# Dense attention of a two-layer block: six matmuls of the identity with residual columns, ahead of the first transposed scores

## The chip, the cores and the metric

The kernel runs as one program on one core of a Trainium2 chip. The metric is the device time of one execution, in microseconds (us). Lower is better. The engines named below are PE (TensorE, the matrix multiplier; PEld is its weight load), DVE (VectorE), ACT (ScalarE), POOL (GpSimd) and SP (SyncE, which here only issues transfers).

## The reference

The program computes two pre-normalised layers on `x` of shape 4 x 1024 x 256: a windowed attention, a mixture of gated experts, a dense attention with a norm behind it, and a mixture with Sinkhorn gates. The change lies in the second attention, which is

```python
def _L1_attn_ref(x, wq, bq, wk, bk, wv, bv, wo, bo, gamma, beta):
    H, D = 16, 16
    Q, K, V = x @ wq + bq, x @ wk + bk, x @ wv + bv
    Q = Q.reshape(B * H, S, D)      # K and V likewise
    scores = jnp.einsum('bqd,bkd->bqk', Q, K) / jnp.sqrt(jnp.float32(D))
    attn = jax.nn.softmax(scores, axis=-1)
    ctx = jnp.einsum('bqk,bkd->bqd', attn, V).reshape(B, S, E)
    out = ctx @ wo + bo + x
    ...
```

The reshape cuts the 1024 x 256 matrix into 16 groups of 64 rows, so that each of the 64 groups (4 x 16) is an attention of 1024 positions with head size 16, without a mask.

## The kernel before, in words

Each part of the network is a phase: a set of programs, one for each engine, that meet only at semaphores. `group_attention` (line 1656) is the phase of the change. Queries and keys come from `project_groups` by way of device memory, as a rounded part and a rest, and stand in SBUF stacked on 48 rows (`ST`) for each of two halves of the 128 partitions (`HR`, 64).

The work is cut into 512 units (`UNITS`: 32 blocks of `UB` = 16). One unit is 128 queries of one group against its 1024 keys. It is handled twice:

- As **scores** (`scores`, line 1885): two matmuls of 48 rows, 128 columns of weights and 512 moving columns, one for each half of the keys. They fill one of two slots (`b_s`, 1024 columns of PSUM each). DVE takes the maximum over the 1024 columns (line 1811). `slot_of` (line 1871) makes PE wait until DVE has read the slot's previous use, two uses ago. After 16 units DVE transposes the block's maxima (line 1818), and SP and POOL copy them by small DMAs into one more row of the queries (lines 1758 and 1790).
- As **transposed scores** (`scores_T`, line 1893): the same products with the keys as weights and 49 rows, the extra row being the negated maxima. The result lies in one of three PSUM banks (`b_t`, `RING` = 3). ACT takes the exponential of it (line 1845), and `weigh` (line 1906) multiplies the values with it: four matmuls of 256 columns, each on 32 columns of the array.

PE's order is written out by the loop at line 1953. At step `s` it does the scores of unit `s`, and the transposed scores of unit `back = s - LAG` with `LAG` = 26. The weighing begins at `back` = 4:

```python
if s < UNITS:
    scores(s, 1).then_inc(use_done, 1)
if 0 <= back < UNITS:
    scores_T(back, 1)
if 4 <= back <= UNITS + 3:
    weigh(back // 2 - 2, back % 2)
```

So steps 0 to 25 hold scores alone, steps 26 to 29 hold scores and transposed scores, and from step 30 on there is the weighing too. At a few places of each pair of blocks (step 65 is the first) `context` and `project` add transposes and a projection, which use the slots as well. Two matmuls of different halves of the rows, a unit's scores and another's transposed scores, run at the same time when they stand next to one another in the order, which is why the order alternates them.

The operands of the added matmul exist already: `g.ident` is the 128 x 128 identity and `g.x` the residual, 32 tiles of 256 columns, both of type fp32. `b_t[s % RING]` is a bank that nothing has used yet at these steps.

Of the kernel before, what the change touches and what calls it, by code (L numbers as in the profile page):

```python
# [54 lines left out]
@contextmanager  # L55
def phase(nc):

    sems = []
    with ExitStack() as e:  # L64
        def semaphore(name):
            sem = e.enter_context(nc.semaphore(name))
            sems.append(sem)
            return sem

        def begin():  # L70
            def start(eng, share):
                for sem in share:
                    eng.sem_clear(sem)
                for sem in share:
                    eng.sem_inc(sem, ONE)

            with nc.Block() as block:  # L77
                @block.sync
                def _(sp):
                    start(sp, sems[0::4])  # L80

                @block.scalar
                def _(act):
                    start(act, sems[1::4])

                @block.vector
                def _(dve):
                    start(dve, sems[2::4])

                @block.gpsimd  # L90
                def _(pool):
                    start(pool, sems[3::4])
            return e.enter_context(nc.Block())

        yield e, semaphore, begin
# [526 lines left out]
def normalised_tiles(nc, g, gate, gate_b, logits, rows_out, xnT_out, shared):  # L622
# [3 lines left out]
    C, HALVES = 4, 2  # L626
    STEPS, TH = T // C, C // HALVES
    with phase(nc) as (e, semaphore, begin):
# [21 lines left out]
        def _(sp):  # L650
# [4 lines left out]
            shared.load_weights(sp, g.ins, 0, shared_in)  # L655
            for i in range(STEPS):
                sp.wait_ge(xn_ready, ONE + C * (i + 1))
# [5 lines left out]
                if i:  # L663
                    sp.wait_ge(lo_ready, ONE + HALVES * i)
                    sp.dma_start(xnT_out[i - 1], parts[:, :, :, C * P * (i - 1):C * P * i].bitcast(F32)).then_inc(parts_kept, 16)
            sp.wait_ge(lo_ready, ONE + HALVES * STEPS)
            sp.dma_start(xnT_out[STEPS - 1], parts[:, :, :, C * P * (STEPS - 1):].bitcast(F32)).then_inc(parts_kept, 16)
            sp.wait_ge(shared_in, ONE + 16 * shared.LOADS)
            sp.wait_ge(chunks_in, ONE + 16 * 2)
            sp.wait_ge(parts_kept, ONE + 16 * STEPS)  # L670
            for u in range(2):
                sp.wait_ge(rows_kept[u], ONE + 16 * (STEPS // 2))

# [982 lines left out]
def group_attention(nc, g, parts, values, qs, ks, v):  # L1656
# [9 lines left out]
    LAG = UB + 10  # L1666
    SETS = 3
    RING = 3
# [2 lines left out]
    RB = UB // 2  # L1671
    CONTEXT_AT, TURN_AT, PROJECT_AT = 7, 13, 18
    LATE = BLOCKS // 2 - 2
    STEPS = UNITS + LAG + UB + 20

    def block_of(b):
# [2 lines left out]
    def score_unit(s):  # L1679

        b, j = s // UB, s % UB
        c, gp, hf = block_of(b)
        return c, j % 2, 2 * gp + j // 2 // HQ, HQ * hf + j // 2 % HQ
# [6 lines left out]
    def step_uses(s):  # L1690

        uses = [("scores", s)] if s < UNITS else []
        pair, at = (s - LAG) // (2 * UB) - 1, (s - LAG) % (2 * UB)
        if 0 <= pair < BLOCKS // 2:
            uses += [("context", pair)] * (at == CONTEXT_AT) + [("project", pair)] * (at == PROJECT_AT)
        return uses

    def transposed_context(back):

        return back // (2 * UB) - 1 if back > UB and back % (2 * UB) == TURN_AT else None  # L1700
# [11 lines left out]
    with phase(nc) as (e, semaphore, begin):  # L1712
# [17 lines left out]
        b_s, b_t, b_o = g.bank2[0:2], g.bank[4:4 + RING], g.bank[7]  # L1730
# [62 lines left out]
        def _(dve):  # L1793
# [6 lines left out]
            def statistics(m):  # L1800
                for t in (first_tile(m), first_tile(m) + 2):
                    nc.vector.bn_stats(g.stats[:, t, :], g.x[:, t, :]).then_inc(stats_ready, 1)

            for s in range(STEPS):
                for kind, arg in step_uses(s):
# [19 lines left out]
                    elif kind == "project":  # L1825
                        t = first_tile(arg)
                        both = g.x[:, t:t + 3:2, :]
                        nc.vector.tensor_tensor(both, slot[:].rearrange("p (h n) -> p h n", h=2)[:, :, 0:D], both, ALU.add).then_inc(use_read, 1)
                        if arg >= LATE:
                            dve.wait_ge(use_read, ONE + use + 1)  # L1830
                            statistics(arg)
                if UNITS <= s < UNITS + LATE:
                    m = s - UNITS
# [36 lines left out]
        def _(pe):  # L1870
            def slot_of(use):
                if use >= 2:
                    pe.wait_ge(use_read, ONE + use - 1)
                return b_s[use % 2]
# [10 lines left out]
            def scores(s, kh):  # L1885

                c, h, n, q = score_unit(s)
                a, rows = c % SLOTS, slice(HR * h, HR * h + ST)
                slot = b_s[use_place["scores", s] % 2]
                return nc.tensor.matmul(slot[:, HALF * kh:HALF * (kh + 1)], qs[a][rows, n, P * q:P * (q + 1)],  # L1890
                                        ks[a][rows, n, HALF * kh:HALF * (kh + 1)], start=True, stop=True)

            def scores_T(back, n):

                w, b, j = 2 * back + n, back // UB, back % UB
                c, gp, hf = block_of(b)
                a, h, kt = c % SLOTS, 1 - j % 2, j // 2
                rows = slice(HR * h, HR * h + ST + 1)
                if j == 0 and n == 0:
                    pe.wait_ge(max_in[0][b % 2], ONE + MAX_IN * (b // 2 + 1))  # L1900
                    pe.wait_ge(max_in[1][b % 2], MAX_IN * (b // 2 + 1))
                bank = ring_bank(ring_place["weights", w])
                nc.tensor.matmul(bank[:], ks[a][rows, 2 * gp + n, P * kt:P * (kt + 1)],  # L1903
                                 qs[a][rows, 2 * gp + n, HALF * hf:HALF * (hf + 1)], start=True, stop=True).then_inc(sT_done, 1)

            def weigh(k, half):

                b, kt = k // RB, k % RB
                c, gp, hf = block_of(b)
                first = HALF // 2 * half  # L1910
                cols = slice(first, first + HALF // 2)
                if kt == 0 and half == 0:
                    pe.wait_ge(o_ready, ONE + b)
                    if b % 4 == 0:
                        pe.wait_ge(v_in[c % SLOTS], ONE + V_IN * (c // SLOTS + 1))
                pe.wait_ge(exp_ready, ONE + NG * (k + 1))
                for h in range(2):
                    for n in range(2):
                        at = BL * (2 * h + n)
                        last = nc.tensor.matmul(b_o[at:at + BL, cols], v[c % SLOTS][:, h, 2 * gp + n, kt, :],  # L1920
                                                probT[k % SETS][2 * h + n][:, cols], start=(kt == 0 and first == 0),
                                                stop=(kt == RB - 1 and first > 0), skip_group_check=True)
                last.then_inc(pv_done, 1)
# [10 lines left out]
            def context_T(m):  # L1934
                bank = ring_bank(ring_place["contextT", m])
                pe.wait_ge(use_read, ONE + use_place["context", m] + 1)
                for n in range(NG):
                    last = nc.tensor.transpose(bank[:, P * n:P * (n + 1)], ctxn[:, n].rearrange("p q d -> p (q d)"), g.ident[:])
                last.then_inc(cT_done, 1)
# [13 lines left out]
            for s in range(STEPS):  # L1953
                back = s - LAG
                if s < UNITS:
                    c = s // (4 * UB)
                    if s == 2 * UB:
                        pe.wait_ge(qk_in[0], ONE + FIRST_IN)
                    elif s % (4 * UB) == 0 and c > 0:
                        first = FIRST_IN if c % SLOTS == 0 else QK_IN  # L1960
                        pe.wait_ge(qk_in[c % SLOTS], ONE + first + QK_IN * (c // SLOTS))
                    slot_of(use_place["scores", s])
                    scores(s, 0)
                if 0 <= back < UNITS:
                    scores_T(back, 0)
                if s < UNITS:
                    scores(s, 1).then_inc(use_done, 1)
                if 0 <= back < UNITS:
                    scores_T(back, 1)
                if 4 <= back <= UNITS + 3:  # L1970
                    weigh(back // 2 - 2, back % 2)
                for kind, arg in step_uses(s):
                    if kind != "scores":
                        other[kind](arg)
                if transposed_context(back) is not None:
                    context_T(transposed_context(back))
# [484 lines left out]
```

## Time and profile before

| what | value |
|---|---|
| median of 3 runs | 2432.5 us |
| the runs | 2428.86, 2432.5 and 2436.8 us |
| profiled execution, its own time | 2439.18 us |
| its span, first to last instruction | 2437.2 us |
| mean granted clock of PE | 0.908 |
| PE busy | 2024.1 us, 83% of the span |
| DVE busy | 1630.2 us, 67% |
| ACT busy | 1116.2 us, 46% |
| the phase of the change | 1375.7 to 2124 us |

A granted clock of 1.00 stands for 2.4 GHz and 0.50 for 1.2 GHz. The busy time of PE counts each matmul with its latency, and overlapping matmuls once. So a PE shown as busy for the whole of a stretch can still have gaps in which no column goes through the array. An fp32 matmul shows up as two MATMUL records.

### The profile page before, as it was taken

How to read it: one execution, taken by the hardware profiler on the slowest of the kernel's cores; microseconds unless marked ns; L12 is line 12 of the kernel's file. 1: busy time of each engine (PE TensorE's matmuls, PEld its weight loads, DVE VectorE, ACT ScalarE, POOL GpSimd, SP SyncE). 2: the span in 40 equal slices, each digit the busy share in tenths (PEclk: the TensorE clock that was granted, in tenths of full speed). 3: DMA queues.
4: the chain of work that ended last, by engine and by line, in shares of the span. 5: the costliest groups of instructions: out<-in, count | busy, mean ns of one | idle time of the engine just before them, and what ended most of it. 6: DMA issues, size and time to landing. Idle time of an engine off the chain costs nothing. (4 is left out here: it accounts for less than half of the span.)

```text
span 2437.2 us, 51300 instructions
## 1 busy us (share of the span) xinstructions
PE 2024.1 (83%) x18407; PEld 1393.6 (57%) x18408; DVE 1630.2 (67%) x2834; ACT 1116.2 (46%) x2169; POOL 452.3 (19%) x608
## 2 busy tenths in 40 slices
PE   2888888669979999989968899999999999835052
PEld 2766766448879999988857533434334343324042
DVE  3666666556735555546644579999999999386953
ACT  1555545333223333332223158888888888611010
POOL 2101001010011111114434112112221122030036
PEclk9999999889989999999989769999999999955566
DMA  2000000192151111113339777745755900031036
GB/s 87 2 0 0 0 0 0 60 336 80 35 182 47 47 47 47 47 43 106 109 114 271 201 51 72 67 46 52 49 47 47 71 2 2 5 104 35 0 112 200
DMA packets 207045, 172.15 MB, mean 71 GB/s; under 512 B 121740, under 2 KB 184808, under 8 KB 204744
## 3 DMA queue, kind: packets, MB, share of 16 engines
q1 hardware_dynamic: 187448, 131.64, 27.8%
q0 software_dynamic: 17744, 26.26, 4.0%
q10 hardware_dynamic: 1728, 12.58, 1.4%
q8 instruction: 79, 1.29, 0.3%
q14 instruction: 46, 0.38, 0.1%
HBM read 106.30 MB, written 63.84 MB: 70 GB/s over the span
## 5 line engine op out<-in xcount | busy, mean ns | idle before, releaser
L1811 DVE TENSOR_REDUCE ga_nmax<-banks 128x1 fp32r<-128x1024 f32 x512 | 615.5, 1219 | 39.8 <-PE banks L1890 38.4
L1845 ACT ACTIVATE ga_probT<-banks 128x512 f32<-128x512 f32 x1024 | 556.7, 597 | 157.6 <-PE banks L1903 105.9
L1890 PE MATMUL banks<-a_ks,a_qs 48*128 48x512 f32 x1024 | 392.3, 466 | 9.3 <-PEq L77 5.3
L1903 PE MATMUL banks<-a_qs,a_ks 49*128 49x512 f32 x1024 | 381.8, 453 | 0.0
L1920 PE MATMUL banks<-ga_probT,a_v 128*32 128x256 f32 x4096 | 332.9, 398 | 6.4 <-ACT ga_o L1851 6.4
L1890 PEld LDWEIGHTS banks<-a_ks,a_qs 48*128 48x128 f32 x1024 | 159.4, 195 | 225.2 <-DVE ga_nmax L1811 158.3
L1321 PEld LDWEIGHTS banks<-rb_xT,rb_own_w 128*128 128x128 f32 x2272 | 267.1, 193 | 8.3 <-issue 3.7
L1321 PE MATMUL banks<-rb_xT,rb_own_w 128*128 128x128 f32 x2272 | 267.9, 276 | 4.1 <-DMA rb_w<-in_L_ffn_rw_dram 3.5
L1790 POOL DMA_DIRECT2D a_qs<-ga_max_rows x256 | 130.8, 519 | 580.6 <-DVE ga_max_rows L1818 539.4
L1296 ACT ACTIVATE rb_silu<-banks,rb_own_b 128x128 f32<-128x128 f32 x284 | 80.9, 367 | 254.9 <-PE banks L1321 254.9
L1920 PEld LDWEIGHTS banks<-ga_probT,a_v 128*32 128x32 f32 x4096 | 81.6, 108 | 198.3 <-ACT ga_probT L1845 151.2
L1101 PE MATMUL banks<-m_xnT,sh_w 128*128 128x512 f32 x768 | 185.0, 400 | 6.4 <-DVE sh_w L896 5.3
L1101 PEld LDWEIGHTS banks<-m_xnT,sh_w 128*128 128x128 f32 x768 | 146.3, 193 | 39.7 <-issue 9.3
L1903 PEld LDWEIGHTS banks<-a_qs,a_ks 49*128 49x128 f32 x1024 | 154.8, 189 | 10.1 <-ACT ga_probT L1845 8.8
L1213 POOL DMA_INDIRECT rb_xb<-normalised_rows,m_source x71 | 67.3, 948 | 467.5 <-PE banks L1315 319.3
L346 DVE TENSOR_REDUCE wa_nmax<-banks 128x4 f32<-128x512 f32 x128 | 86.9, 679 | 97.3 <-PE banks L543 97.3
L1246 DVE SCALAR_TENSOR_TENSOR rb_gluT<-banks,rb_own_b,rb_silu 128x128 f32<-128x128 f32 x284 | 79.9, 344 | 91.8 <-PE banks L1321 91.8
L1343 PE MATMUL banks<-rb_w,rb_gluT 128*128 x568 | 135.6, 382 | 1.4 <-DVE rb_gluT L1246 1.4
L414 ACT ACTIVATE wa_probT<-banks 128x512 f32<-128x512 f32 x128 | 76.4, 597 | 130.6 <-PE banks L555 130.6
L1343 PEld LDWEIGHTS banks<-rb_w,rb_gluT 128*128 128x128 f32 x568 | 103.3, 192 | 12.9 <-issue 1.6
L555 PE MATMUL banks<-ident,wa_prob 128*128 128x128 f32 x512 | 85.8, 291 | 25.1 <-ACT wa_prob L407 25.1
L407 ACT ACTIVATE wa_prob<-wa_ex 128x512 f32<-128x512 f32 x128 | 80.5, 629 | 51.1 <-DVE wa_ex L348 50.1
(288 smaller groups left out, 3031.7 us busy)
## 6 DMA issues: line engine op xcount, KB each, us to landing
m_xnT<-xnT_parts ACTq DMA_DIRECT2D x12, 1024.0 KB, 4.8
sorted_out<-rb_yb SPq DMA_DIRECT2D x71, 128.0 KB, 1.7
xnT_parts<-np_parts SPq DMA_DIRECT2D x8, 1024.0 KB, 9.2
m_w<-in_L_ffn_rw_dram SPq DMA_DIRECT2D x2, 4096.0 KB, 21.6
values<-pg_v SPq DMA_DIRECT2D x16, 512.0 KB, 3.1
a_v<-values SPq DMA_DIRECT2D x16, 512.0 KB, 9.1
a_qs<-queries_rounded SPq DMA_DIRECT2D x28, 256.0 KB, 8.5
a_ks<-keys_rounded SPq DMA_DIRECT2D x28, 256.0 KB, 9.6
```

The lines of the kernel that those rows point to most:

```text
L346: nc.vector.tensor_reduce(nmax[k][:], sc, axis=AX.X, op=ALU.max, negate=True).then_inc(max_ready, 1)
L555: last = nc.tensor.transpose(b_pt[k][:, P * j:P * (j + 1)], prob[k][:, j, :], g.ident[:])
L1101: last = nc.tensor.matmul(bank[m % 2][:], w[a][:, k, P * m:P * (m + 1)], xnT[s][:, b, k, :], start=(k == 0 and a + b == 0), stop=(k == KD ...
L1296: last = nc.scalar.activation(silu[:, m, :], b_p1[:, P * m:P * (m + 1)], ACT.Silu, bias=own_b[s][:, 0, m:m + 1])
L1321: last = nc.tensor.matmul(bank[:, P * m:P * (m + 1)], w[:, k, P * m:P * (m + 1)], xT[s][:, k, :], start=(k == 0), stop=(k == KD - 1))
L1343: last = nc.tensor.matmul(b_y[:, 0:D], gluT[:, m, :], flat[:, bass.ds(n * KH + m, 1), :].rearrange("p o d -> p (o d)"), start=(m == 0), st ...
L1790: nc.gpsimd.dma_start(dst, src).then_inc(max_in[1][b % 2], 16)
L1811: nc.vector.tensor_reduce(nmax[b % 2][:, at:at + 1], slot[:], axis=AX.X, op=ALU.max, negate=True).then_inc(use_read, 1)
L1845: nc.scalar.activation(probT[k % SETS][2 * h + n][:], b_t[ring_place["weights", w] % RING][:], ACT.Exp, scale=SCALE).then_inc(exp_ready, 1)
L1890: return nc.tensor.matmul(slot[:, HALF * kh:HALF * (kh + 1)], qs[a][rows, n, P * q:P * (q + 1)], ks[a][rows, n, HALF * kh:HALF * (kh + 1)] ...
L1903: nc.tensor.matmul(bank[:], ks[a][rows, 2 * gp + n, P * kt:P * (kt + 1)], qs[a][rows, 2 * gp + n, HALF * hf:HALF * (hf + 1)], start=True, ...
L1920: last = nc.tensor.matmul(b_o[at:at + BL, cols], v[c % SLOTS][:, h, 2 * gp + n, kt, :], probT[k % SETS][2 * h + n][:, cols], start=(kt == ...
```

## The change

At each of the steps 20 to 25 (`LAG - BUSY <= s < LAG`), behind the second half of the scores, PE multiplies the identity by 512 columns of the residual, in fp32, into the bank `b_t[s % 3]`. No semaphore is attached. The bank is overwritten later by transposed scores, and nothing reads what the matmul wrote. The results are the same.

```diff
@@ -1671,6 +1671,7 @@
     RB = UB // 2
     CONTEXT_AT, TURN_AT, PROJECT_AT = 7, 13, 18
     LATE = BLOCKS // 2 - 2
+    BUSY = 6
     STEPS = UNITS + LAG + UB + 20
@@ -1965,6 +1966,8 @@
                     scores_T(back, 0)
                 if s < UNITS:
                     scores(s, 1).then_inc(use_done, 1)
+                if LAG - BUSY <= s < LAG:
+                    nc.tensor.matmul(b_t[s % RING], g.ident[:], g.x[:, 0:2, :].rearrange("p t d -> p (t d)"), start=True, stop=True)
                 if 0 <= back < UNITS:
                     scores_T(back, 1)
```

## Rows read from the trace of the kernel before

**Rows 1.** The page: the granted clock in 40 slices, and the costliest group.

```profile
PEclk9999999889989999999989769999999999955566
...
L1811 DVE TENSOR_REDUCE ga_nmax<-banks 128x1 fp32r<-128x1024 f32 x512 | 615.5, 1219 | 39.8 <-PE banks L1890 38.4
```

**Rows 2.** Busy time by stretch; the last row is that of line 1811 alone.

```profile
core 0: us, PE busy (x) PEld busy (x) DVE busy (x) ACT busy (x) POOL busy (x), PEclk, DMA share, GB/s
...
1376.00:1401.00 25.00, 22.15 (x40) 9.22 (x40) 22.48 (x20) 1.02 (x1) 3.28 (x7) 0.50 0.79 105
...
1415.00:1446.00 31.00, 31.00 (x178) 9.97 (x176) 18.02 (x16) 15.95 (x30) 4.08 (x8) 0.50 0.91 58
1446.00:1487.00 41.00, 40.59 (x392) 15.67 (x388) 38.77 (x36) 34.97 (x66) 8.18 (x16) 1.00 0.59 67
...
1446.00:1487.00 41.00, 37.53 (x32) 1.00 0.59 67
```

**Rows 3.** Timeline of steps 20 and 21: start, us, engine, work, count, idle before.

```profile
1401.16 2.35 PE L1890 MATMUL banks<-a_ks,a_qs 48*128 48x512 f32 x4 [0.18 <-DVE ga_nmax L1811]
...
1403.70 0.49 PEld L1890 LDWEIGHTS banks<-a_ks,a_qs 48*128 48x128 f32 x2 [0.91 <-DVE ga_nmax L1811]
```

**Rows 4.** Timeline of the step at 1418.15, clock at 0.50, with weighing.

```profile
1417.14 1.08 PE L1920 MATMUL banks<-ga_probT,a_v 128*32 128x256 f32 x8
...
1417.57 0.65 PE L1920 MATMUL banks<-ga_probT,a_v 128*32 128x256 f32 x4
...
1418.15 0.29 PEld L1890 LDWEIGHTS banks<-a_ks,a_qs 48*128 48x128 f32 x1 [0.81 <-issue]
...
1419.30 0.20 PEld L1920 LDWEIGHTS banks<-ga_probT,a_v 128*32 128x32 f32 x8 [0.65 <-issue]
...
1420.31 0.79 PE L1890 MATMUL banks<-a_ks,a_qs 48*128 48x512 f32 x1
```

**Rows 5.** Timeline of the same kind of step with the clock at 1.00.

```profile
1448.38 0.64 PE L1920 MATMUL banks<-ga_probT,a_v 128*32 128x256 f32 x8 [0.21 <-ACT ga_o L1851]
1448.95 0.18 PEld L1890 LDWEIGHTS banks<-a_ks,a_qs 48*128 48x128 f32 x1 [0.41 <-issue]
...
1449.61 0.64 PE L1920 MATMUL banks<-ga_probT,a_v 128*32 128x256 f32 x8
```

**Rows 6.** Timeline: where step 26 and step 45 start.

```profile
1408.76 0.79 PE L1890 MATMUL banks<-a_ks,a_qs 48*128 48x512 f32 x1 [0.18 <-DVE ga_nmax L1811]
...
1446.20 0.50 PE L1890 MATMUL banks<-a_ks,a_qs 48*128 48x512 f32 x1
```

**Rows 7.** Timeline of an fp32 matmul of 512 columns elsewhere, at either clock.

```profile
480.38 0.59 PE L757 MATMUL banks<-np_xnT,np_gw 128*128 128x512 f32 x1
...
480.38 1.02 PE L757 MATMUL banks<-np_xnT,np_gw 128*128 128x512 f32 x2
...
487.30 1.06 PE L757 MATMUL banks<-np_xnT,np_gw 128*128 128x512 f32 x1
...
487.30 1.91 PE L757 MATMUL banks<-np_xnT,np_gw 128*128 128x512 f32 x2
```

**Rows 8.** Who waited for whom, PE, 1376 to 2080: us in total, times, longest.

```profile
PE banks L1920 <- ACT ga_o L1851: 6.2, 30, 0.2
PE banks L1890 <- PEq L77: 5.3, 1, 5.3
PE banks L1890 <- DVE ga_nmax L1811: 3.9, 15, 1.4
```

**Rows 9.** Busy time by stretch at a rise and a fall (columns as rows 2).

```profile
466.60:469.60 3.00, 0.97 (x4) 0.68 (x4) 1.78 (x5) 0.00 (x0) 0.00 (x0) 1.00 0.00 0
470.00:473.00 3.00, 0.00 (x0) 0.00 (x0) 1.73 (x10) 1.60 (x2) 0.00 (x0) 0.50 0.00 0
...
1259.00:1261.50 2.50, 2.50 (x7) 1.96 (x7) 0.00 (x0) 0.00 (x0) 2.50 (x1) 0.50 0.00 0
1262.00:1265.00 3.00, 3.00 (x37) 2.56 (x37) 1.56 (x4) 1.26 (x4) 2.94 (x2) 1.00 0.48 160
```

## The prediction

> **What bounds the kernel now.** I read the page first [rows 1]. The costliest group is the maximum on DVE: 512 times 1.219 us, 615.5 us of a phase of some 748. The row of granted clocks dips to 7 and 6 just where this phase begins. Next comes the busy time by stretch [rows 2]. PE ran at 0.50, which is 1.2 GHz, from the phase's start to 1446 us, and at 1.00, 2.4 GHz, after it. The timelines then say what limits each part.
>
> Steps 0 to 29, up to 1415 us, are bound by DVE. Two steps take 2.54 us, from 1401.16 to 1403.70, so one takes 1.27. PE stands there until DVE has read the slot [rows 3]. The low clock costs nothing here, since at full clock the steps are no quicker: 32 maxima in 41 us are 1.28 us a step, with DVE busy for 38.77 us of the 41 [rows 2].
>
> From step 30 on, at 0.50, PE is the bound. The step runs from 1418.15 to 1420.31, 2.16 us [rows 4], and DVE is busy for only 18.02 us of 31 [rows 2]. It splits into 1.15 us from the start of the scores to that of the weighing (1419.30) and 1.01 us from there to the next scores. At full clock the same parts take 0.66 and 0.57 us, 1.23 in all, and DVE is the bound again [rows 5]. What a higher clock can win lies in this regime alone. Step 26 starts at 1408.76 us and step 45 at 1446.20 [rows 6]: 19 steps in 37.4 us. At 1.27 us each they would take 24.1. So **13.3 us** is all that a clock at 1.00 could give back in the profiled execution.
>
> **The change part by part.** It removes and moves nothing and adds no wait. It adds six matmuls, each with its weight load, in order on PE. No DMA and no other engine is touched.
>
> *One added matmul.* The trace has its shape, fp32 with 128 rows and 512 columns, at line 757. Two records start 1.91 - 1.06 = 0.85 us apart at 0.50, and 1.02 - 0.59 = 0.43 us apart at 1.00 [rows 7]. So the two records of one matmul keep the array for 1.70 or 0.86 us. The changeover I take from the weighing, which stands at the same place in a step. Its two rounds start 0.43 us apart (1417.57 less 1417.14) and so make up 0.86 of its 1.01 us; 0.15 is changeover [rows 4]. The added part is then 1.70 + 0.15 = 1.85 us at 0.50. At 1.00 the changeover can be no more than that 0.15, which gives about 1.0.
>
> *One of the six steps.* The next scores stand behind the added matmul in PE's order. DVE can't hide it: it works beside it, but then lacks the next unit. At 0.50 a step becomes 1.15 + 1.85 = 3.00 us in place of 1.27, which is **1.73 us** more. At 1.00 it becomes 0.66 + 1.0 = 1.66, which is 0.39 more. The cover is what PE now waits in such a step. It is the 1.27 less 1.15, so 0.12 us, and the 1.73 has it taken off already.
>
> *Six of them.* At the low clock throughout it is 6 x 1.73 = 10.4 us, the upper bound. At full clock throughout it is 6 x 0.39 = 2.3 us, the lower. With a rise after two or three steps it is 2.5 x 1.73 + 3.5 x 0.39 = 5.7 us.
>
> Could the weight loads be cheaper? At each change between scores and weighing PEld stood idle for 0.65 or 0.81 us, and loaded only when the matmuls before it were ending [rows 4]. The Trainium skill ("TensorE: Matmul & The Clock Gate", Step-by-step: what each phase is for) says that PE pulls a weight load ahead of running matmuls where the row groups don't conflict or the background buffer is free. By that rule both changeovers would go (0.15 us here, and 1.15 less 0.85 ahead of the scores), a step would take 2.55 us, and the six would cost 6 x 1.28 = 7.7 us. The rows speak against it between operands of different shape, and I keep 10.4.
>
> *Maxima and loads.* The block's maxima leave at step 32 and are wanted at step 42; a delay ahead of both shifts both. Nowhere in the phase does PE wait for a DMA: its waits are for ACT, for the start and for DVE [rows 8]. SP's and POOL's queues get more time, not less. If later steps ran at full clock, the ten steps would last 12.7 us, as they do in all later blocks, where no such wait shows either. So this costs nothing, and if the cover went, it would be a wait ahead of the first transposed scores of a block. The banks: nobody waits for what the added matmuls write, and no semaphore moves. That is nothing, too.
>
> *The clock.* This is the open term. At 1259 us fp32 matmuls of 128 rows back to back were at 0.50, and from 1262 us the clock was at 1.00 [rows 9]. From 1415 to 1446 us, in contrast, PE counted as busy for the whole of 31 us, in equal steps of 2.16 us, and the clock stayed at 0.50 [rows 2]. It rose at 1446 us with nothing new in the steps [rows 6]. So 31 busy us of this kind can pass without a rise. The new steps are a mixture: in 3.00 us they pass columns for 1.70 us through 128 rows and for 0.85 us through 48. The equal steps pass them, in 2.16 us, for 0.86 us through 128 rows and for 0.85 us through 97 (scores beside transposed scores). Neither is clearly the denser. I take it that the six, 18 us at most, are like the 31 us more often than like the back-to-back ones.
>
> Then there is what follows. Steps 26 to 29 have no weighing and are bound by DVE. At full clock PE would pass columns for 0.43 us in each 1.27 us there, for some 5 us. The nearest row is a fall: with 0.97 busy us of 3 at 466 us, the clock was at 0.50 from 470 us on [rows 9]. So a clock raised by the six would probably be lost again before step 30, where it first is worth something.
>
> **Sum.** Against the profiled execution it is 2439.18 + 10.4 = 2449.6 us. That execution (2437.2 us of span, 2.0 us around it) is 6.7 us above the median of the three runs. The likeliest reason is a late rise of the clock, as nothing in the steps ties the rise to 1446 us. The added cost does not depend on that, so I put it on the median: 2432.5 + 10.4, so **2443 us**.
>
> **The rivals.**
> - *A, my forecast: the clock stays low through the six steps.* 2443 us. For it: 31 us of PE-bound steps at 0.50. Against it: that stretch did end in a rise. Chance 0.50.
> - *B, the clock rises during the six and falls again in steps 26 to 29.* It costs 5.7 us and gives nothing back: 2438 us. For it: dense fp32 matmuls brought the clock up at 1262 us. Chance 0.25.
> - *C, the clock rises and stays; the other side.* It costs 5.7 us. Back come 13.3 us in the profiled execution; in the median run at least 13.3 - 6.7 = 6.6, if its 6.7 us less come from an earlier rise. That is 2424.9 to 2431.6 us, and I take 2430. It decides at steps 26 to 29: if the clock is still at 1.00 at step 30, the change gains. Against it: the fall at 470 us. Chance 0.20. The Trainium skill has this as a rule (same page, The HAM clock gate): activity releases the throttle, and idleness brings it back. By that rule alone, with PE busy from step 20 on, C would be the forecast. The 31 us busy at 0.50 disagree with it, as far as busy is what the profile counts.
> - *D, nothing happens*: the matmuls fit into PE's waiting, or aren't there. 2432.5 us. Against it: PE waits for 0.18 us ahead of the scores [rows 3]. Chance 0.05.
>
> **How the numbers follow.** Runs of this kernel lie some 4 us to either side of the median. About 0.3%, 7.3 us, is what a measurement can tell from no change. Slower by more means above 2439.8 us: four fifths of A and two fifths of B, 0.50. Faster by more means below 2425.2: two fifths of C, and a little for a rise that is worth more than I think, 0.10. The other 0.40 is between. The range goes from 2428, C's middle less 2 us, to 2450, A with its rise as late as in the profiled execution. It leaves out the better part of C and the worst of A.
>
> **What would show it.** In the changed kernel's trace the scores of steps 20 to 26 should start 3.0 us apart, with the added records 0.85 us apart, and step 26 should start 10 us later, near 1419 us. The clock should be at 0.50 up to there, and the steps from 30 on should take 2.16 us until a rise at some other time. If step 26 comes only 4 to 7 us late, the clock rose, and its row over the 5 us behind tells B from C. If the scores stay 1.27 us apart, it is D. If the steps take 2.6 us with the records 0.85 us apart, the weight loads were pulled ahead.

## The result and the profile after

| kernel | median | lowest and highest | runs |
|---|---|---|---|
| before | 2432.41 us | 2427.82, 2440.7 | 19 |
| changed | 2445.52 us | 2440.98, 2454.58 | 19 |

The ratio is 1.0054, with a 95% interval of 1.0042 to 1.0066, which is 10.2 to 16.1 us. The change is slower. The forecast was 2443 us. The profiled execution took 2447.26 us, against 2439.18 before.

The page of the changed kernel, first its span, the clock in 40 slices and the costliest group (lines behind the change have moved by 1 to 3):

```profile
span 2445.3 us, 51324 instructions
...
PEclk9999999889989999999989769999999999955566
...
L1812 DVE TENSOR_REDUCE ga_nmax<-banks 128x1 fp32r<-128x1024 f32 x512 | 615.8, 1220 | 48.0 <-PE banks L1891 46.7
```

Against [rows 1], the dip in the clock is where it was, and DVE's work is the same. What has grown is DVE's wait for the scores, from 38.4 to 46.7 us, so by 8.3. The two spans differ by 8.1, so this wait accounts for the difference of the profiles.

Busy time by stretch, the columns being those of [rows 2]:

```profile
1375.00:1400.00 25.00, 22.12 (x40) 9.48 (x40) 22.18 (x20) 1.28 (x1) 3.19 (x8) 0.50 0.74 105
1400.00:1419.00 19.00, 18.82 (x25) 5.99 (x24) 8.87 (x8) 0.00 (x0) 1.17 (x3) 0.50 0.96 69
1419.00:1425.50 6.50, 6.06 (x21) 3.09 (x20) 4.70 (x4) 4.48 (x9) 0.00 (x0) 0.50 0.00 1
1425.50:1450.00 24.50, 24.50 (x142) 7.90 (x140) 14.24 (x14) 12.67 (x24) 4.08 (x8) 0.50 0.76 54
1450.00:1491.00 41.00, 40.59 (x391) 15.69 (x388) 38.75 (x36) 34.93 (x67) 8.19 (x16) 1.00 0.47 59
```

The second row holds the six steps: PE is busy for 18.82 of 19 us, DVE only for 8.87, and the clock is at 0.50. It is still at 0.50 in the thin steps 26 to 29 behind them (third row) and for another 24.5 us of weighing (fourth), as it was in the kernel before.

The timeline of step 21 in the changed kernel, with the columns of [rows 3]; each of the two records of the added matmul (L1970) has a line:

```profile
1403.60 0.50 PEld L1891 LDWEIGHTS banks<-a_ks,a_qs 48*128 48x128 f32 x2 [1.50 <-DVE ga_nmax L1812]
1403.60 1.22 PE L1891 MATMUL banks<-a_ks,a_qs 48*128 48x512 f32 x2
1404.74 0.50 PEld L1970 LDWEIGHTS banks<-x,ident 128*128 128x128 f32 x2 [0.65 <-issue]
1404.75 1.22 PE L1970 MATMUL banks<-x,ident 128*128 128x512 f32 x1
1404.85 1.23 DVE L1812 TENSOR_REDUCE ga_nmax<-banks 128x1 fp32r<-128x1024 f32 x1 [1.93 <-PE banks L1891]
1405.76 1.06 PE L1970 MATMUL banks<-x,ident 128*128 128x512 f32 x1
1406.75 0.50 PEld L1891 LDWEIGHTS banks<-a_ks,a_qs 48*128 48x128 f32 x2 [1.50 <-DVE ga_nmax L1812]
```

The step takes 3.15 us (1403.60 to 1406.75), 1.15 of it to the start of the added matmul and 2.00 for the added matmul. Its two records start 1.01 us apart (1404.75 and 1405.76), and the next scores start 0.99 us after the second. DVE now waits for 1.93 us ahead of this maximum.

Counted from the phase's first matmul, step 20 starts at 25.38 us in both kernels. Step 26 starts at 32.98 us before and at 44.30 us after: **11.3 us** later, 6 x 1.89. Step 30 is still 11.3 us late. The last scores (step 511) start at 701.92 and 710.49 us, only 8.6 us apart. The missing 2.7 us are the clock's: before, it rose 70.3 us after the phase's start, when 15 of the slow steps of 2.16 us had passed, and in the changed kernel 75.3 us after it, when 12 had.

The medians differ by 13.1 us, and 11.3 lies inside the interval. The lowest of 19 runs is 13.2 us above the lowest of before. So the times show no sign of a rise during the six steps that would have made them cheap. The steps themselves were seen in one execution, and single runs of a kernel lie up to 14 us apart, so a rise in a few of the 19 runs is not ruled out.

### The profile page after: what moved, and what is told of

Same layout as the page of the kernel before. It is cut to its first block and busy times, and to the rows that moved or that the text cites. A ratio compares the mean times of both kernels' runs of the same rounds, so it can differ in the third digit from the quotient of the medians.

```text
span 2445.3 us, 51324 instructions
## 1 busy us (share of the span) xinstructions
PE 2031.3 (83%) x18419; PEld 1394.8 (57%) x18420; DVE 1630.2 (67%) x2834; ACT 1116.9 (46%) x2169; POOL 454.3 (19%) x608
## 5 line engine op out<-in xcount | busy, mean ns | idle before, releaser
L1812 DVE TENSOR_REDUCE ga_nmax<-banks 128x1 fp32r<-128x1024 f32 x512 | 615.8, 1220 | 48.0 <-PE banks L1891 46.7
L1904 PEld LDWEIGHTS banks<-a_qs,a_ks 49*128 49x128 f32 x1024 | 154.1, 188 | 10.4 <-ACT ga_probT L1846 8.8
```

The source lines that it names most:

```text
L1812: nc.vector.tensor_reduce(nmax[b % 2][:, at:at + 1], slot[:], axis=AX.X, op=ALU.max, negate=True).then_inc(use_read, 1)
```

## The experiments

Each kernel was timed beside the kernel before, on the same chip, and ratios are against it. The first three experiments and the one with 512 columns in steps 30 to 32 ran where the kernel before has a median of 2432.77 us, the others on a chip where it takes 2461.3 or 2462.39; medians forecast for those are to be read as differences. Starts of steps are counted from the phase's first matmul, in one profiled execution each, and compared with the 32.98 us (step 26) and 38.05 us (step 30) in the profile of the kernel before. Step 20 starts at 25.38 or 25.39 us in every kernel that adds nothing ahead of it. What the clock did was seen in these single executions alone.

**Twelve steps in place of six.**

```diff
-    BUSY = 6
+    BUSY = 12
```

> Twelve steps with an added matmul (14 to 25) in place of six. Theory A (the clock stays at 0.50 and each such step costs what the changed kernel's trace shows, 3.15 us against 1.27): 12 x 1.885 = 22.6 us up to step 26 in the profile, that is 11.3 us more than the changed kernel, median about 2455 to 2457 us. Rival B (more of the same steps do raise the clock): the later ones take 1.7 us, the delay at step 26 is 10 to 15 us and the median is 2440 to 2450. If the 1.8 us by which the medians differ beyond 11.3 belong to each added matmul, the median is 2458.5 or more.

Measured: step 26 starts at 55.62 us, 22.6 us late, and every one of the twelve steps takes 3.15 us. Median 2457.09 us, ratio 1.0094 (1.0073 to 1.0116). By stretch:

```profile
1397.00:1435.00 38.00, 37.84 (x49) 11.98 (x50) 16.15 (x15) 0.00 (x0) 4.17 (x8) 0.50 0.67 49
1435.00:1446.00 11.00, 10.56 (x53) 4.68 (x52) 7.72 (x8) 7.19 (x14) 0.75 (x2) 0.50 0.01 2
1446.50:1500.00 53.50, 53.09 (x516) 20.39 (x516) 51.26 (x47) 46.22 (x87) 11.04 (x22) 1.00 0.82 73
```

For 38 us PE was busy with these steps alone and the clock stayed at 0.50. More of the same did not raise it, and the price is 1.89 us for each matmul. The medians differ by 24.3 us, 1.7 more than the 22.6; with six matmuls it was 13.1, 1.8 more than the 11.3. So what lies beyond the steps did not grow from six matmuls to twelve.

**A quarter of the columns.**

```diff
-nc.tensor.matmul(b_t[s % RING], g.ident[:], g.x[:, 0:2, :]..., start=True, stop=True)
+nc.tensor.matmul(b_t[s % RING][:, 0:P], g.ident[:], g.x[:, 0, 0:P], start=True, stop=True)
```

> The added fp32 matmul has 128 columns in place of 512, at the same six steps. Theory A (column time plus a changeover of 0.29 us): a step takes 1.15 + 0.43 + 0.29 = 1.87 us, 0.60 over 1.27, so 3.6 us up to step 26; median 2435 to 2438 us. Rival (the cost is that of a weight load and changeover and hardly depends on columns): 7 us or more. If PE's idle time hid a short one: under 1 us.

Measured: step 26 at 36.62 us, 3.6 us late. Median 2435.6 us, ratio 1.001 (0.9994 to 1.0026). Its timeline, with the second record of the added matmul in the fourth line:

```profile
1402.57 1.22 PE L1891 MATMUL banks<-a_ks,a_qs 48*128 48x512 f32 x2
1403.72 0.50 PEld L1970 LDWEIGHTS banks<-x,ident 128*128 128x128 f32 x2 [0.65 <-issue]
1403.72 0.80 PE L1970 MATMUL banks<-x,ident 128*128 128x128 f32 x2
1404.09 0.42 PE L1970 MATMUL banks<-x,ident 128*128 128x128 f32 x1
1404.44 0.50 PEld L1891 LDWEIGHTS banks<-a_ks,a_qs 48*128 48x128 f32 x2 [0.23 <-issue]
```

The added part is 0.72 us here (1403.72 to 1404.44) and 2.00 us with 512 columns. So 384 columns cost 1.28 us, which at 1.2 GHz is four times through the array. At that rate 128 columns make up 0.43 of the 0.72 us, and what is left beside the columns is 0.29 us, as with 512. It has two parts in both kernels. The second record starts late: 0.37 us after the first (1403.72 and 1404.09) where the columns take 0.21, and 1.01 us in place of 0.85 with 512. That is 0.16 us. The other 0.14 lies between the last columns and the next scores. Most of the cost of the 512-column matmul is the columns', since 0.29 of its 2.00 us does not depend on them.

**Three in each of the six steps.**

```diff
+                    for _ in range(3):
+                        nc.tensor.matmul(b_t[s % RING], g.ident[:], ..., start=True, stop=True)
```

> Three of the 512-column matmuls in each of the six steps, so that columns go through all 128 rows for 5.1 of 6.6 us. Theory: this is dense enough to raise the clock, as the back-to-back fp32 matmuls at 1259 us were; then it falls again in or just behind steps 26 to 29, where PE has only the scores. Delay at step 26: one or two steps at +5.3 us and the rest at +2.1, 15 to 20 us; from step 30 on 2.16 us a step again, and the median is 2448 to 2455. Rival C (a raised clock stays): the same delay, but from step 30 on 1.25 us a step, and about 9 us less. Rival A at its strictest (nothing of this kind raises it): delay 32 us, median 2465.

Measured: step 26 at 47.87 us, 14.9 us late. Median 2438.89 us, ratio 1.0024 (1.0009 to 1.0039). By stretch:

```profile
1403.60:1407.70 4.10, 3.99 (x6) 1.79 (x7) 2.41 (x3) 0.00 (x0) 0.83 (x2) 0.50 0.03 5
1408.00:1426.00 18.00, 18.00 (x43) 6.95 (x41) 6.12 (x5) 0.00 (x0) 0.00 (x0) 1.00 1.22 69
1426.00:1431.00 5.00, 3.84 (x21) 1.76 (x20) 4.04 (x4) 4.21 (x8) 0.00 (x0) 1.00 0.01 2
1431.00:1480.00 49.00, 48.59 (x474) 18.31 (x472) 47.73 (x45) 42.65 (x80) 12.30 (x24) 1.00 0.73 66
```

By the medians, eighteen added matmuls cost less than six: the clock rose within the first of these steps. In this execution it stayed at 1.00 through the thin steps too, against my expectation, and the steps from 30 on took 1.23 us. At step 511 this kernel was level with the kernel before (702.14 and 701.92 us), in which the clock had risen late.

**Two in each of the six steps** (one profiled execution, no median).

```diff
+                    for _ in range(2):
+                        nc.tensor.matmul(b_t[s % RING], g.ident[:], ..., start=True, stop=True)
```

> Two of the 512-column matmuls in each of the six steps: columns for 4.3 us of 4.86 at 0.50. If it takes more than the change's one and three were plenty, this places the border. Theory: rises within the six steps; step 26 is 10 to 16 us late and the steps from 30 on take 1.23 us. Rival: no rise, 21.5 us late.

Measured: step 26 at 42.75 us, 9.8 us late, which is less than with one a step. By stretch:

```profile
1400.50:1404.90 4.40, 4.22 (x7) 1.67 (x6) 2.73 (x3) 0.00 (x0) 1.17 (x3) 0.50 0.03 4
1405.50:1418.00 12.50, 12.50 (x30) 4.78 (x30) 6.12 (x5) 0.00 (x0) 0.00 (x0) 1.00 1.44 78
1418.00:1422.00 4.00, 3.24 (x17) 1.46 (x16) 2.94 (x3) 3.13 (x6) 0.00 (x0) 1.00 0.86 49
1422.50:1428.50 6.00, 5.90 (x33) 2.10 (x36) 4.16 (x6) 3.50 (x8) 0.72 (x2) 0.50 0.01 3
1429.00:1480.00 51.00, 50.59 (x492) 19.47 (x492) 48.78 (x45) 43.83 (x83) 11.10 (x22) 1.00 0.77 72
```

With two a step the clock rose, in the first step again. It fell in step 29 and rose again 6.8 us later. At 1.00 a step takes 2.57 us here and 3.43 with three, so one matmul more costs 0.86 us.

**Four in step 25 alone.**

```diff
+                if s == LAG - 1:
+                    for _ in range(4):
+                        nc.tensor.matmul(b_t[s % RING], g.ident[:], ..., start=True, stop=True)
```

> Four of the 512-column matmuls in step 25 alone, none elsewhere: the same columns as two thirds of the change, but back to back. Theory (what raises the clock is that columns go through all rows without the scores between them, and a clock so raised stays through steps 26 to 29): 7.1 us at 0.50, less what falls behind the rise, so step 26 is 4 to 7 us late; steps from 30 on take 1.23 us; step 511 in the profile lies 6 to 9 us before that of the kernel before, and the median is 2429 to 2433 us, with a smaller spread. Rival (the raised clock is lost where only scores run): step 26 late by the same, steps from 30 on at 2.16 us until a later rise; median 2437 to 2441 us.

Measured: step 26 at 38.11 us, 5.1 us late. On this chip the kernel before has a median of 2461.3 us, and this one of 2461.94; the ratio is 0.9999 (0.9981 to 1.0018). By stretch:

```profile
1411.00:1416.50 5.50, 5.50 (x8) 2.32 (x9) 3.26 (x3) 0.00 (x0) 0.00 (x0) 0.50 1.44 72
1417.00:1423.00 6.00, 4.85 (x22) 2.06 (x22) 3.77 (x4) 3.94 (x8) 0.00 (x0) 1.00 1.44 69
1424.00:1460.00 36.00, 36.00 (x204) 11.68 (x196) 20.79 (x18) 18.51 (x35) 4.08 (x8) 0.50 0.60 42
1461.50:1500.00 38.50, 38.29 (x366) 15.35 (x363) 36.39 (x33) 32.43 (x61) 8.18 (x16) 1.00 0.68 75
```

This is rival B in this execution. The clock rose within the burst and fell again in step 30, and then came 37.6 us at 0.50, with the same steps of 2.16 us as in the kernel before. Step 511 started 6.4 us later than in the profile of before, and nothing was gained. But this execution is the slowest of the twelve (2477.01 us; the fastest took 2456.24), so the clock may have held in others. Over all runs it is a draw.

**Two in each of the six, and 256 columns in each of steps 26 to 29.**

```diff
+                    if LAG <= s < LAG + 4:
+                        nc.tensor.matmul(b_s[use_place["scores", s] % 2][:, 0:D], g.ident[:], g.x[:, 0, 0:D], start=True, stop=True)
```

> As the kernel with two matmuls in each of the six steps (there the clock rose in step 20, fell in step 29 or 30 and rose again 7 us later), plus 256 columns in each of steps 26 to 29. Theory: the fall came from the thin steps 26 to 29; with the columns it stays at 1.00 from the rise in step 20 or 21 to the end of the phase, and step 34 comes no later than 57 us after the phase's start. Rival (the fall has nothing to do with what these steps pass): it falls again near step 30.

Measured: the rise came in step 20 again and no fall after it; step 34 starts at 53.12 us. Median 2464.73 us beside 2462.39, ratio 1.001 (0.9993 to 1.0027).

```profile
1407.00:1411.00 4.00, 3.91 (x6) 1.67 (x6) 2.40 (x3) 0.00 (x0) 0.84 (x2) 0.50 0.02 2
1411.50:1424.00 12.50, 12.50 (x30) 4.86 (x30) 6.13 (x5) 0.00 (x0) 0.00 (x0) 1.00 1.43 80
1424.00:1430.00 6.00, 5.96 (x28) 2.76 (x27) 3.96 (x4) 3.77 (x8) 0.00 (x0) 1.00 0.69 41
1430.00:1480.00 50.00, 49.59 (x480) 18.78 (x477) 48.73 (x45) 43.59 (x82) 12.32 (x24) 1.00 0.72 65
```

With columns in the thin steps (third row, 5.96 busy us of 6 against 3.24 of 4 without) the clock held. It fits the theory, though in the median it brought no gain. It is one execution, and the kernel with three a step held without them, so it makes the thin steps the likely cause of the falls and not the proven one.

**None before the weighing, 512 columns in each of steps 30 to 32.**

```diff
+                    if LAG + 4 <= s < LAG + 4 + BUSY:    # BUSY = 3
+                        nc.tensor.matmul(b_s[use_place["scores", s] % 2][:, 0:HALF], g.ident[:], ..., start=True, stop=True)
```

> No matmul in the last six steps of scores; instead one of 512 columns ahead of the scores in each of steps 30, 31 and 32, where the weighing has begun. Theory: what matters is that the clock be raised where the steps behind it are dense enough to keep it. It rises during or just after these three steps and stays. Cost 3 x 2.0 us at 0.50, less after the rise, about 4 to 5 us; back come the cold steps up to the old rise (13.3 us in the profile of before, about half of that in the median). Median 2427 to 2433 us, and the spread of the runs is smaller. Rival (added matmuls raise nothing here, or not before they end): 6 us slower than before, 2438 us.

Measured, from scores to scores: step 30 takes 4.17 us and step 31 3.21; the clock rose in step 31, 46.3 us after the phase's start, and stayed:

```profile
1416.00:1425.50 9.50, 9.32 (x34) 3.04 (x32) 4.20 (x5) 4.05 (x8) 0.00 (x0) 0.50 1.30 68
1426.00:1480.00 54.00, 53.59 (x510) 20.43 (x510) 50.84 (x47) 45.73 (x86) 12.27 (x24) 1.00 0.79 69
```

The third added matmul started just behind the rise. Step 33 starts 4.1 us later than before (48.66 and 44.53 us), step 45 7.0 us earlier (63.42 and 70.42). The last scores start at 694.93 us, 7.0 us earlier than in the profile of before. The median is 2433.22 us, ratio 0.9997 (0.9983 to 1.0011). Put here, the matmuls buy what the change was after; in the median run they cost as much as they bring. The runs do lie closer together: 2429.46 to 2436.9 in 12, against 2426.08 to 2445.16 in 29.

**256 columns in each of steps 30 to 33.**

```diff
+                    if LAG + 4 <= s < LAG + 8:
+                        nc.tensor.matmul(b_s[use_place["scores", s] % 2][:, 0:D], g.ident[:], g.x[:, 0, 0:D], start=True, stop=True)
```

> One fp32 matmul of 256 columns ahead of the scores in each of steps 30 to 33, nothing before them. Theory: a cold step becomes 2.16 + 0.85 + 0.2 = 3.2 us, and together with the weighing that is dense enough to raise the clock within one to two steps; behind the rise a step takes 1.9 us in place of 1.25. Cost 2.5 to 4 us, against 7 us that the cold steps cost the median run of the kernel before: ratio 0.997 to 0.999. In the profile step 34 lies 2 to 4 us ahead of the 46.7 us after the phase's start that it has in the kernel before, or at the same place, and the steps behind it take 1.23 us. Rival (256 columns are too few, or the rise is lost again): 4 x 1.05 = 4.2 us slower, ratio 1.0015 or more.

Measured: a miss. The four steps cost 4.6 us together (from scores to scores 3.31 us in place of 2.16), all at 0.50. The clock rose only two steps behind them, 53.3 us after the start, and step 34 is 4.6 us late. The median is 2467.79 us, ratio 1.0017 (1.0 to 1.0034), as the rival had it, though the interval only just reaches no change.

**The clock kept from the phase before.**

```diff
             for s in range(2):
                 project(STEPS - 1, s)
+            for _ in range(3):
+                nc.tensor.matmul(b_t[0][:], g.ident[:], xnT[1][:].rearrange("p k q -> p (k q)"), start=True, stop=True)
...
+                if s < LAG:
+                    nc.tensor.matmul(b_t[s % RING][:, 0:192], g.ident[:], g.x[:, 0, 0:192], start=True, stop=True)
```

> Three 512-column matmuls at the end of the phase before, where PE waits for 5.3 us and the other engines are not done for another 2 to 3 us, and one of 192 columns in each of steps 0 to 25. Theory: the clock is then at 1.00 when the scores begin, and each step still fits into DVE's 1.27 us (0.66 + 0.32 + 0.2), so nothing is paid and the 13 us of the profiled execution come back: median 2424 to 2427 us. Rival (the clock falls all the same in the 2.6 us that still are idle, or with the scores): the small matmuls then cost 0.8 us a step, 20 us, median 2450 or more.

Measured: the rival. Median 2478.62 us beside 2461.3, ratio 1.0063 (1.0038 to 1.0089).

```profile
1371.00:1375.50 4.50, 2.67 (x6) 0.89 (x6) 0.63 (x1) 0.00 (x0) 0.00 (x0) 1.00 0.59 216
1376.00:1378.70 2.70, 2.49 (x9) 1.34 (x10) 1.68 (x2) 1.28 (x1) 0.19 (x2) 1.00 0.34 78
1379.00:1429.00 50.00, 50.00 (x98) 23.95 (x98) 29.99 (x26) 0.00 (x0) 4.18 (x8) 0.50 0.75 70
```

The three matmuls in the gap did bring the clock at 1.00 across the boundary of the phases. It fell in step 2 of the scores, 2.6 us after the phase's start, and from then on each small matmul made a step of 2.09 us out of one of 1.27. Step 26 is 19.3 us late (52.24 us).

## Why the prediction was right

*What bounds the kernel.* Right. The cost lies in DVE's wait for the scores in the six steps, and all work of the phase behind them is shifted.

*One added matmul.* The mechanism was right, and one term was too small. The columns cost what line 757 had said: 1.71 of the 2.00 us. But beside them I put 0.15 us, and it is 0.29. The 0.15 from the weighing is about right for the change to the next scores (0.14). What I left out is the 0.16 us by which the second record starts late: I had written that the records would start 0.85 us apart, and they start 1.01 apart. At line 757 a matmul of the same shape stood ahead, and here the scores do. The rows of before have the same delay in the scores themselves, whose second matmul starts 0.60 us after the first (1418.15 in [rows 4], and the line below), where the columns take 0.43:

```profile
1418.75 0.62 PE L1890 MATMUL banks<-a_ks,a_qs 48*128 48x512 f32 x1
```

The two rounds of the weighing, with 32 columns of weights a load, start 0.43 us apart without such a delay. The scores and the added matmul load 128 columns of weights twice within the first 0.50 us. In the burst of four, whose records begin at 1413.10 us, the delay shows once alone: the next loads start at 1414.11, 1414.96 and 1415.82 us, 1.01 and then 0.85 us apart. That the second record waits for its load wherever nothing of the same shape ran ahead fits all these rows, but no run separates it. The step was forecast at 3.00 us and took 3.15; six of them were put at 10.4 and took 11.3 us.

*The weight loads.* Right to trust the rows. The load of the identity starts 0.65 us after the load before it has ended, when the scores are ending. The load for the next scores starts after 1.50 idle us. The rule of the Trainium skill ("TensorE: Matmul & The Clock Gate", Step-by-step: what each phase is for), that PE pulls weight loads ahead, does not show at either changeover in this trace; the 7.7 us that followed from it would have been 3.6 too few.

*Maxima and loads, banks.* Right: the delay of 11.3 us at step 26 is 11.3 at step 30, and no wait on a DMA has come.

*The clock through the six steps.* Rival A was right in all that was seen: 18 steps of this kind in two profiles and the lowest of 19 runs speak for it. Against two or three a step, the single one leaves the clock alone. The Trainium skill's "activity releases the throttle" (same page, The HAM clock gate) agrees with the rise with two a step at 1405 us and with the burst at 1416 us. It fails where I doubted it, when activity is read off as PE's busy time: 37.84 busy us of 38 left the clock at 0.50.

*What follows the six steps.* The fall that I argued from one row is seen in two of four executions in which the clock was raised ahead of the thin steps (two a step, the burst). It was absent in one without added columns there (three a step) and in the one with them. "Probably lost" was about right as a chance.

*The sum.* Put on the profiled execution, 2439.18 + 10.4 gave 2449.6, and it took 2447.26. The added steps cost 0.9 us more than thought, and a rise three slow steps earlier gave back 2.7; the remaining half a microsecond lies outside the phase. On the median, 2443 was forecast and 2445.52 measured; 0.9 of these 2.5 us are the matmul's late second record, and the other 1.6 are within the interval; no run shows what they are. That two or three a step do raise the clock shows how near rival B was: the row at 1262 us, which spoke for it, was right about denser work, and that the 31 us of equal steps were the nearer row was a guess at even odds that came out.

## What to carry to other kernels

A matmul that nobody waits for is free only in time that PE has to spare at its present clock. Here that was 0.12 us a step at 0.50, and the filler made PE the bound at 3.15 us a step. Filler meant to raise the clock should be tried dense or not at all, since one matmul a step cost 11.3 us and raised nothing while three a step raised the clock at once, and it should stand where the steps behind it are dense too. Even then it brought nothing in the median here. In the best place, steps 30 to 32, it cost 4.1 us up to step 33, and by the medians the slow steps that it saves are worth no more than that.

## What the runs showed that I had not expected

The cheapest of the three counts was not the smallest: up to step 26, one a step cost 11.3 us, two a step 9.8, three a step 14.9.

PE's busy time hides behind which steps the clock rises. Rows with 37.84 of 38 us and 36.00 of 36 us busy stood at 0.50, while 4.22 of 4.40 and 5.50 of 5.50 were followed by 1.00.

Runs of one and the same kernel differ, and the profiles show one reason, the time at which the clock rises. In seven of them the weighing ran at 0.50 from step 30 on, or within a microsecond of it, with no filler beside it (the kernel before, the changed one, twelve steps, a quarter of the columns, two a step, the burst, the clock kept from the phase before). There the rise came 6 to 39 us after the start of step 30, and each of the slow steps costs 0.9 us. What decides when it comes stays open.
